# Attention of a decoder layer on one core: a new order of key scores, means, squares, variances and the inverse

## The reference

```python
kv = _ln(x, kvn_w, kvn_b) @ kv_w + kv_b
q = (_ln(x, qn_w, qn_b) @ q_w + q_b)
q, k = _rotary(q, x, rh_w, rh_b), _rotary(k, x, rh_w, rh_b)
qn, kn = _ln(q, ln_w, ln_b), _ln(k, ln_w, ln_b)      # over each head's 32
scores = jnp.einsum('bhqd,bhkd->bhqk', qn, kn) / np.sqrt(HD)
attn = jax.nn.softmax(scores, axis=-1)
a = jnp.einsum('bhqk,bhkd->bhqd', attn, v)
...
x = _layernorm(x + a @ out_w + out_b)
```

## Time and profile before

| what | value |
|---|---|
| runs shown | 2009.02, 2010.94, 2013.51 us |
| median | 2010.94 us |
| the profiled execution's own time | 2008.56 us |
| its span from first to last instruction | 2006.8 us |
| PE, DVE, ACT, POOL busy over the span | 88, 73, 63, 43% |
| granted TensorE clock, mean | 0.954 |
| attention's units | first exponential at 93.29 us, last ends at 1063.3 us |

### The profile page before, as it was taken

How to read it: one execution, slowest core, us unless ns; L and a number is a source line. 1 busy time by engine, 2 the same in 40 slices (tenths; PEclk the granted TensorE clock), 3 DMA queues, 4 the chain that set the end, 5 groups by cost and what they waited for, 6 DMA issues and landing times. The chain is left out here.

```text
span 2006.8 us, 26502 instructions
## 1 busy us (share of the span) xinstructions
PE 1763.3 (88%) x8648; PEld 1322.4 (66%) x8648; DVE 1467.1 (73%) x2915; ACT 1263.7 (63%) x2674; POOL 866.4 (43%) x802
## 2 busy tenths in 40 slices
PE   6788898888898898888888999999998999999972
PEld 5556665656566565665536888888886777777751
DVE  7678687786777867777664777777764688888875
ACT  3388787887878868788683232322224667777764
POOL 3678678686876868768621222222220000000000
PEclk9799999999999999999978999999998999999986
DMA  4222132322323223222252111111121011111111
GB/s 154 54 84 64 54 105 64 100 59 67 93 63 107 52 67 97 59 86 55 72 167 111 63 39 47 53 53 63 63 89 56 10 42 64 64 64 64 42 42 63
DMA packets 86184, 141.06 MB, mean 70 GB/s; under 512 B 16544, under 2 KB 19616, under 8 KB 86048
## 3 DMA queue, kind: packets, MB, share of 16 engines
q1 hardware_dynamic: 86048, 139.37, 22.9%
HBM read 63.82 MB, written 25.17 MB: 44 GB/s over the span
## 5 line engine op out<-in xcount | busy, mean ns | idle before, releaser
L527 DVE TENSOR_REDUCE a_neg_max<-a_max 128x1 fp32r<-128x512 f32 x512 | 340.5, 685 | 151.5 <-PE a_max L912 150.4
L797 ACT ACTIVATE a_probs<-a_exp 128x512 f32<-128x512 f32 x512 | 297.3, 607 | 172.2 <-PE a_exp L932 172.0
L776 ACT ACTIVATE a_max<-a_max,a_neg_max 128x512 f32<-128x512 f32 x512 | 346.1, 687 | 17.5 <-DVE a_neg_max L527 16.7
L912 PE MATMUL a_max<-a_stack 96*128 96x512 f32 x512 | 220.5, 457 | 86.1 <-ACT a_max L776 77.9
L369 POOL TENSOR_TENSOR a_rstd<-a_rstd,a_minus_half 128x16 f32<-128x16 f32 x64 | 185.9, 2905 | 81.6 <-DVE a_rstd L511 81.5
L1728 POOL TENSOR_TENSOR f_yrstd<-f_yrstd,f_minus_half 128x4 f32<-128x4 f32 x8 | 11.0, 1374 | 473.4 <-DVE f_yrstd L1747 473.4
L912 PEld LDWEIGHTS a_max<-a_stack 96*128 96x128 f32 x512 | 98.9, 196 | 176.1 <-ACT a_max L776 128.9
L932 PE MATMUL a_exp<-a_stack 100*128 100x512 f32 x512 | 195.9, 416 | 12.2 <-ACT a_probs L797 9.0
L887 PE MATMUL a_t<-a_w_hi,a_zT_hi 128*128 128x384 f32 x500 | 179.6, 359 | 18.6 <-DVE a_v L492 15.6
L888 PE MATMUL a_t<-a_w_lo,a_zT_hi 128*128 128x384 f32 x500 | 172.3, 345 | 0.0
L889 PE MATMUL a_t<-a_w_hi,a_zT_lo 128*128 128x384 f32 x500 | 171.8, 344 | 0.0
(11 more groups left out here) (282 smaller groups left out, 4812.0 us busy)
## 6 DMA issues: line engine op xcount, KB each, us to landing
a_stack<-a_nT_hi SPq DMA_DIRECT2D x512, 64.0 KB, 2.0
a_stack<-a_nT_lo SPq DMA_DIRECT2D x256, 64.0 KB, 2.0
a_z<-x SPq DMA_DIRECT2D x8, 1024.0 KB, 7.9
a_y<-x SPq DMA_DIRECT2D x8, 1024.0 KB, 5.6
r_xn<-x SPq DMA_DIRECT2D x8, 1024.0 KB, 5.7
r_cn<-ctx SPq DMA_DIRECT2D x8, 1024.0 KB, 7.9
x<-r_xn SPq DMA_DIRECT2D x16, 512.0 KB, 2.8
f_xn<-x SPq DMA_DIRECT2D x8, 1024.0 KB, 5.6
```

Source lines behind the costliest of these rows:

```text
L527: nc.vector.tensor_reduce(neg_max[:, t, ROW + h:ROW + h + 1].bitcast(F32R), bank_max[i % NB][:, :], AX_X, ALU.max, negate=True).then_inc(m ...
L776: nc.scalar.activation(bank_max[i % NB][:, :], bank_max[i % NB][:, :], ACT.Exp, bias=neg_max[:, t, ROW + h:ROW + h + 1], accum_out=sums[:, ...
L797: nc.scalar.activation(probs[:, kt % 2, h, :], bank_exp[i % 2][:, :], ACT.Exp).then_inc(exp_done, 1)
L912: mm(bank_max[i % NB][:, :], stack[0:ROW, par, h, t * P:(t + 1) * P], stack[0:ROW, par, HG + h, :], start=True, stop=True).then_inc(score_ ...
```

## The change

It has six parts.

1. `KS_DONE` and `WEIGH_AT` are one list for all units: two, five, seven, nine key scores by steps 0 to 3, then one a step, all 16 by step 10. Weighs stand at steps 3, 5, 8 and 12. PE interleaves key scores and projection items in every unit, and in step 0 two items go first.
2. Both head means of U + 3 stand at step 14 ahead of `spread_max`; squares of U + 2 at steps 0 and 1 ahead of the exponentials; variances at steps 0 and 1.
3. Per tile, `x_stats` is split in two (`x_variance` and `x_stats`) at steps 3, 6, 8 and 9; `x_final` and `x_rstd` move from g = 3 to the next batch's g = 0 (steps 3 and after head_norm); `x_shift` moves to step 7 and `x_norm` to steps 8 to 11.
4. `invert` stands at step 5, `save_inverse` at step 14 (13 for g = 3).
5. In units with g > 0 the two banks of the projection are swapped, and PE's turns stand at steps 8 and 9 with their waits and the steps of `turn_high` and `turn_low` to match.
6. POOL adds the bias between `centre` and `head_norm`.

```diff
-KS_DONE = ((2, 5, 7, 8, 9, 10, 11, 12, 13, 14, 15, 16, 16, 16, 16, 16),
-           tuple(min(4 * (i + 1) // 3, T * HG) for i in range(16)))
+KS_DONE = (2, 5, 7, 9, 10, 11, 12, 13, 14, 15, 16, 16, 16, 16, 16, 16)
-WEIGH_AT = ((3, 5, 9, 13), (5, 7, 10, 13))
-TURN_AT, SAVE_AFTER = ((8, 11), (8, 10)), ((0, 1, 4, 7), (0, 1, 4, 7))
+WEIGH_AT = (3, 5, 8, 12)
+TURN_AT, SAVE_AFTER = ((8, 11), (8, 9)), ((0, 1, 4, 7), (0, 1, 4, 7))
-X_NORM_AT, STATS_AFTER, FINAL_AFTER, SHIFT_AFTER = (6, 7, 8, 9), (5, 7), 9, 4
-VAR_AFTER, SQUARE_AT = (2, 3), (1, 2)
-TURN_HIGH_AT, TURN_LOW_AFTER = ((9, 12), (9, 11)), ((10, 13), (10, 12))
-INVERT_AFTER, INVERSE_AT, INVERSE_SAVE_AT, ATTN_HIGH_AT, ATTN_LOW_AFTER = 6, 11, 12, 0, 0
+X_NORM_AT, STATS_AFTER, FINAL_AFTER, SHIFT_AFTER = (8, 9, 10, 11), (3, 6, 8, 9), 3, 7
+VAR_AFTER, SQUARE_AT = (0, 1), (0, 1)
+TURN_HIGH_AT, TURN_LOW_AFTER = ((9, 12), (9, 10)), ((10, 13), (10, 11))
+INVERT_AFTER, INVERSE_AT, INVERSE_SAVE_AT, ATTN_HIGH_AT, ATTN_LOW_AFTER = 5, 11, (14, 14, 14, 13), 0, 0
...
# POOL's unit
                     for s in range(2):
                         centre(U + 2, s)
+                if g >= 2:
+                    for t in range(2 * (g - 2), 2 * (g - 1)):
+                        add_bias(b, t)
+                if left >= 2:
                     for s in range(2):
                         head_norm(U + 2, s)
-                if g == 3 and more:
-                    x_rstd(b + 2)
+                if g == 0 and b >= 1 and b + 1 < B:
+                    x_rstd(b + 1)
...
# DVE's unit
-                    if left >= 2 and i == 0:
-                        for s in range(0 if U == 0 else 1, 2):
+                    if U == 0 and i == 0:
+                        for s in range(2):
                             head_mean(U + 2, s)
...
-                        x_stats(b + 2, 2 * (g - 2) + STATS_AFTER.index(i))
-                    if g == 3 and more and i == FINAL_AFTER:
-                        x_final(b + 2)
+                        t, half = divmod(STATS_AFTER.index(i), 2)
+                        (x_stats if half else x_variance)(b + 2, 2 * (g - 2) + t)
+                    if g == 0 and 1 <= b < B - 1 and i == FINAL_AFTER:
+                        x_final(b + 1)
...
                     if i == SAVE_MAX_AT and left >= 3:
-                        head_mean(U + 3, 0)
+                        for s in range(2):
+                            head_mean(U + 3, s)
                     if i == SAVE_MAX_AT and left >= 1:
                         spread_max(U + 1, (g + 1) % 2)
...
# ACT's unit
+                    for s in range(2):
+                        if left >= 2 and i == SQUARE_AT[s]:
+                            square(U + 2, s)
-                    for m in within(KS_DONE[g > 0], i):
+                    for m in within(KS_DONE, i):
                         exps(U, m)
...
-                    if i == INVERSE_SAVE_AT:
+                    if i == INVERSE_SAVE_AT[g]:
                         save_inverse(U)
-                    for s in range(2):
-                        if left >= 2 and i == SQUARE_AT[s]:
-                            square(U + 2, s)
...
# PE: projection's waits and banks, turns' wait
-                        if t == 1:
+                        if t == 0 and one == 2:
                             pe.wait_ge(nTlo_done, 2 * (U + 1) + 2)
...
-                project(U + 3, (g + 3) % G, t, k, bank_t[t % one])
+                project(U + 3, (g + 3) % G, t, k, bank_t[0 if g == 0 else (t + 1) % 2])
...
-                    pe.wait_ge(qkv_saved, T * (U + 3) + (4 if g == 0 else 3 + s))
+                    pe.wait_ge(qkv_saved, T * (U + 3) + (4 if g == 0 else 4 - s))
...
# PE's unit
-                    keys = list(within(KS_DONE[g > 0], i))
-                    if g > 0 or i == 0:
-                        for m in items:
-                            project_item(b, g, m)
-                        for m in keys:
-                            key_scores(U, g % 2, m)
-                    else:
-                        for n_item in range(max(len(items), len(keys))):
-                            if n_item < len(keys):
-                                key_scores(U, g % 2, keys[n_item])
-                            if n_item < len(items):
-                                project_item(b, g, items[n_item])
-                    if i in WEIGH_AT[g > 0]:
-                        weigh(U, g, WEIGH_AT[g > 0].index(i))
+                    keys = list(within(KS_DONE, i))
+                    ahead = 2 if i == 0 else 0
+                    for m in items[:ahead]:
+                        project_item(b, g, m)
+                    for n_item in range(max(len(items) - ahead, len(keys))):
+                        if n_item < len(keys):
+                            key_scores(U, g % 2, keys[n_item])
+                        if n_item + ahead < len(items):
+                            project_item(b, g, items[n_item + ahead])
+                    if i in WEIGH_AT:
+                        weigh(U, g, WEIGH_AT.index(i))
```

More of the change, by code:

```diff
@@ L396, in unit @@
                         rotate(U + 3, s)
-                if g >= 2:
-                    for t in range(2 * (g - 2), 2 * (g - 1)):
-                        add_bias(b, t)
             x_rstd(0)
@@ L436, in _, with x_variance @@
             dve.wait_ge(split_done, 1)
-            def x_stats(b, t):
+            def x_variance(b, t):
                 if t == 0:
@@ L442, in x_stats @@
                 nc.vector.bn_stats(stats[:, t, :], z[:, t, :])
+            def x_stats(b, t):
                 nc.vector.scalar_tensor_tensor(scratch[:, :], z[:, t, :], 1.0, rh_w[:, :], ALU.mult, ALU.mult,
@@ L603, in unit @@
                         t = SAVE_AFTER[g > 0].index(i)
-                        save_qkv(U + 3, (g + 3) % G, t, bank_t[0 if g == 0 else t % 2])
+                        save_qkv(U + 3, (g + 3) % G, t, bank_t[0 if g == 0 else (t + 1) % 2])
                     if i == ATTN_LOW_AFTER and counts(U):
@@ L702, in _ @@
             for t in range(3):
+                x_variance(1, t)
                 x_stats(1, t)
@@ L714, in _ @@
                 save_qkv(1, 1, t, bank_t[t % 2])
+            x_variance(1, 3)
             x_stats(1, 3)
```

## The result

The changed kernel takes 2031.38 us (median of 4 runs, 2029.13 to 2034.9), against 2010.6 for the kernel before on the same chip: ratio 1.0101, 95% interval 1.0063 to 1.0138. It is slower by 21 us where 12 less were forecast, and outside the range.

A forecast was written before the change was run, and what follows sets the result against it. No engine is full; PE and ACT take turns at being late. Seven full batches sum to -24.5 + 21D, -11.9 with D = 0.6; 2008.56 - 11.9 + 2.4 = 1999 us, range for 8 in 10: 1974 to 2017.

The forecast's parts named there:

- Exp 0's wait for the keys: At a unit's head, PE's first key could start 1.06 us sooner; exp 0's wait gone or under 0.3.
- The head of g = 1: Square 0 waits for a late centre and holds exp 0 and key 2: +1.2 us a batch.
- D: Head's delay of exp 2 and key 2 in units 2, 3 and next 0: 0.6 us taken, 0 to 2.1 possible.
- 3.6 against 4.9: ACT's holes in a g > 0 unit, walked after against before: 1.3 us less a unit, -3.9 a batch.
- 7 x (1.2 + 3D): Costs at the heads over seven full batches: 1.2 us at g = 1, D at three others.
- 7 x (-3.9 - 0.8): Gains over seven full batches: 3.9 us from g = 1, 2 and 3, 0.8 from g = 0 units.
- The tail: At a unit's end, weigh 3 moves earlier: holes of 0.15 and 0.55 us, transposes 1.3 after query 15.
- g = 0: PE-bound units gain 0.8 us each; x moments moved there cost 0 beside idle DVE and POOL.
- Batch 7: The batch with fewer stages, taken as 0 +- 2 us.
- The clock: Half-clock stretches in thin PE work at the tail: taken as 0, ends 10 us gained or 16 lost.
- The head locks: Rival: in every unit square 0 waits for a late centre, the spread waits out centre 1; 2031 us, chance 0.18.
- nothing moves: Rival: holes at exps 0 and 1 reappear at exps 5, 8 and 11; 2007 to 2015 us, chance 0.14.

The follow-up runs named there:

- part 2 undone: The changed kernel with means, squares and variances at the head put back in their old places: 2005.82 us, 0.9972.
- the added matmuls: The changed kernel plus seven useless matmuls in each g > 0 unit, three ahead of query 12, four ahead of the inverse's transposes: 2020.18 us, 1.0033.
- before with its matmuls: The kernel before plus six useless matmuls ahead of query 15 in each g > 0 unit: 2004.7 us, 0.9963.
- part 2 undone and the same x moments and matmuls: The changed kernel with means, squares and variances put back, plus seven useless matmuls in each g > 0 unit: 1999.1 us, 0.9917.
- Part 3 alone: The kernel before with only the x moments moved (statistics split, x_final and x_rstd in the next g = 0 unit): 2021.28 us, 1.0051.
- part 1 alone: The kernel before with only the keys ahead (new key and weigh lists, keys and items interleaved): 2036.45 us, 1.0131.
- part 2 alone: The kernel before with only both means at step 14, squares ahead of the exponentials and variances at steps 0 and 1: 2050.11 us, 1.0192.
- part 1 undone: The changed kernel with key scores, weighs and interleaving as before: median 2025.04 us, 1.0026, executions in two groups.

## Why the prediction was wrong

**Right.** Exp 0's wait for the keys is gone and exp 1 is 0.48 behind (0.5 to 0.8 said). A wait stands at exp 5 as said; the one at exp 8 is small, and exp 11 waits more. The head of g = 1 was to cost 1.2, by a square that waits for the centre; it costs 1.1 against the kernel before (3.32 from 2.21), and square 0 waits 1.59 for POOL.

**Right by luck: D.** It was taken as 0.6, and against part 2 undone the heads of g = 2, 3 and 0 cost 0.51, 0.52 and 0.83. But it was built from 0.3 for a late square and 0.3 for part of a lock. At most heads of g = 2 and 3 the square does not wait and the spread is not held up: the 0.5 is the square's own length between the copy and exp 0. The 0.3 was also worked out wrongly: a rotation that ends 0.9 before exp 0, then a centre of 1.05 and a square of 0.6, end 0.75 late and not 0.3.

**The step that failed: "3.6 against 4.9" of holes, 1.3 us less a unit, -3.9 a batch.** ACT's slots were right, 22.2 us. In the undisturbed g = 1 unit of batch 2 the holes are 26.98 - 22.2 = 4.8: before exp 4 0.30 (said 0.25), exp 5 1.00 (1.05), exp 6 0.28 (0.27), exp 8 0.23 (0.70), exp 11 1.04 (0.65), the tail 0.90 (0.70); then those that had no place in the sum: 0.38 before sum 0, and some 0.6 in pieces of 0.12 to 0.18 around the inverse copy, square 0 and exp 0. Most holes that I named were there at nearly their size. They make 3.75 together, against 3.6 said; exp 8 was too high and exp 11 too low. What failed was the balance: the list leaves out 1.05 us of holes, while the 4.9 that it was set against was measured whole. Such a unit was to take 26.4 (27.1 - 1.3 + 0.6 for D); undisturbed, g = 1 takes 26.98, as before (26.96 in batch 2), and g = 2 and 3 take 27.54 and 27.91 (with the added matmuls), more than before with its matmuls (26.81 and 27.47). These have 5.3 and 5.7 of holes. Sums 13 and 14 of g = 2 and sum 13 of g = 3 wait there for DVE, which has the x moments in steps 3 to 9 of these units. That these are the cause was not tried by itself, and they are not enough for it in g = 3: with part 2 undone and the same x moments and matmuls such a unit takes 26.37.

The runs with part 2 undone split the sum of the prediction in two, and show that it is this half that failed. Part 2 was to cost 7 x (1.2 + 3D), 21 us with D = 0.6; it costs 26 us without and 23 with the added matmuls (the intervals leave 9 and 6). All the rest was to give 7 x (-3.9 - 0.8), -33 us; it gives -6 (0.9972 against 1) and -9 (0.9917 against 0.9963), with 5 and 7 left open. So 24 to 27 of the 32 us between forecast and result are the gain of the keys, the tail and the g = 0 units, which was not there. That part 2 came out near its price is luck in part, too: 5.5 of its 23 us are the first unit, which the sum left out.

**The tail** was costed by its holes alone (0.15 and 0.55; measured 0.14 and 0.76). "The inverse copy fills ACT's wait for the transposes" was wrong: sum 15 ends as the transposes do, so the copy lies on the chain, and the transposes come 1.65 after query 15 (the second of two at 410.63, 0.23 apart), not 1.3.

**g = 0:** "-0.8", with the x moments at nothing beside idle DVE and POOL. Measured +2.0 a batch with the 1.1 of the next head in it, so +0.9. Part 3 alone adds 2.7 to these units (some of it with the clock, see above); the cover was idle time in total, not at the place. Which of its pieces does it was not separated.

**The first unit** was not in the sum. Square 0 now stands ahead of the very first exponential and waits 7.47 us for POOL:

```profile
95.28 0.63 ACT L767 ACTIVATE a_turn<-a_n 128x512 f32<-128x512 f32 x1 [7.47 <-POOL a_n L362]
95.82 1.06 ACT L804 ACTIVATE a_probs<-a_exp 128x512 f32<-128x512 f32 x2
```

It starts at 95.82; before at 93.29, with part 2 undone at 90.93. Batch 7, taken as 0 +- 2, costs 3.3.

**The clock** was taken at 0 with ends of -10 and +16; by the two kernels with added matmuls it is +6, but the intervals leave 9 either way.

In the profiled runs: prologue +2.5, batch 0 +1.9, batches 1 to 6 +18.3 (762 against 743), batch 7 +3.3, the rest -1.5, in all +24.5.

**The rivals.** "The head locks" gave 2031, the measured time, but not by what happened. The spread was to wait out centre 1; it never does (L536 over the loop, in ns; compare). It is the other way round:

```profile
L536 DVE CAST a_stack<-a_stack x26: 690/691/692, 259.8 to 1043.9; 4x1024 fp32r<-4x1024 f32 x26
```

```profile
L362 POOL TENSOR_TENSOR a_n<-a_n,a_mean x50: 1046/1298/1586, 258.7 to 1017.1; 128x512 f32<-128x512 f32 x50
```

At every head of batches 1 to 6 the spread starts 0.02 to 0.05 us ahead of centre 1 and keeps its 0.69, and centre 1 takes 1.55 to 1.59 in place of 1.05. So the two still meet, and POOL pays, off the chain of exp 0, as only square 1 needs centre 1.

The means' scaling does meet POOL, with a median of 424 ns in place of 176, but never 1294; D stayed near 0.6 and not 2.1. A spread that is held up shows with part 2 alone (1.71, above), among these two. What came true is "nothing moves" for the units with g > 0, which eats the gain, plus a first unit, g = 0 units that were to gain, and perhaps a clock.

**Open:** why part 1 makes g = 0 units longer (42.6 alone, median), how much of part 1's cost is the clock, what part 6 does, why a g = 3 unit pays 1.4 for part 2, and why in the order of part 2 the wait turns up again in g = 1 when the squares are moved back.

## What to carry to other kernels

When two queues hand work to each other, a wait that is removed at one place is won only if the whole period is recomputed; set a measured total against a walked total only after the walk has reproduced the total of the kernel before. An operation of another pipeline stage put ahead of the first operation of a unit cost at least its own length (0.5 us) at each head here, and in the first unit the whole latency of its inputs (5.5 us). Change one part at a time: of four parts here only the tail gained (0.6%), and it lost that again beside the keys. A test that is to take the clock away is read by the granted clock of its own trace first: in two of the kernels with added matmuls it was hardly better than without.

## What the runs showed of the hardware

Useless matmuls where TensorE waits made three kernels faster: -0.68% (changed kernel; lower level 111.5 to 61.4 us of the attention), -0.37% (before; 72.3 to 54.8) and -0.55% (part 2 undone; 93.6 to 62.1). With part 1 alone, six ahead of query 15 cost 1.3%. A stretch at half clock costs by its place: 1.2 us in a unit of the kernel before, 1.4 (28.95 against 27.54) where two queries stand behind the slowed weigh. The same program can come out at either of two clocks: with part 1 undone, 2000.4 to 2005.4 us at a mean of 0.956 to 0.958, and 2024.6 to 2027.0 at 0.940 to 0.942.

The Trainium skill ("SBUF — State Buffer", Who interferes with whom) lets some VectorE operations and GpSimd block each other. The traces agree where they overlap, and the one that starts later is the one that gets longer: the cast takes 1.71 in place of 0.69 us when POOL is at work as it starts (part 2 alone), and keeps 0.69 when it starts 0.02 to 0.05 us ahead of the centre, which then takes 1.55 to 1.59 in place of 1.05 (changed kernel).
